# Two block turns of the expert loop written as products in 64-column halves, and a reordered start of the attention stage

## The reference, cut to what matters

```python
x = x + _L0_xattn_ref(ctx_1024, _layernorm(x))     # alignment of x to the context by dynamic time warping
x = x + _L0_ffn_ref(_layernorm(x), gate, W1, b1, W2, b2)   # 16 experts, 3 per row
x = x + _L1_xattn_ref(ctx_1024, _layernorm(x), mask, ...)  # attention over context and x
x = x + _L1_ffn_ref(_layernorm(x), Wg, bg, Wi, Wo, A, B)   # 4 low-rank experts on a shared base
```

```python
hidden = relu(x @ W1[e] + b1[e])        # 512 -> 1024
expert_out = hidden @ W2[e] + b2[e]     # 1024 -> 512
out = sum over the 3 chosen e of gate_topk[e] * expert_out
```

## Time and profile before

| what | us |
|---|---|
| median of 3 runs | 1135.21 |
| lowest and highest run | 1132.46, 1137.16 |
| the profiled execution, its own time | 1130.05 |
| its span | 1128.4 |
| TensorE busy | 1023.9 (91%) |
| first turn_hidden of the loop to the last | 363.66 to 709.69 |
| first seam instruction of TensorE | 720.85 |

### The profile page before, as it was taken

One profiled execution on the slowest core, in us unless ns is written; L12 is line 12 of the kernel. 1 busy time (PEld: TensorE's weight loads), 2 busy tenths in 40 slices (PEclk: granted clock), 3 DMA queues, 4 the chain that ended last, 5 costly groups with the idle time before them and its releaser, 6 DMA issues. The chain is left out here.

```text
span 1128.4 us, 19664 instructions
## 1 busy us (share of the span) xinstructions
PE 1023.9 (91%) x6339; PEld 637.5 (57%) x6340; DVE 521.8 (46%) x2007; ACT 349.0 (31%) x947; POOL 257.5 (23%) x327
## 2 busy tenths in 40 slices
PE   8966679973996999999999999799999989999997
PEld 7963234542465666666666666554466655555553
DVE  6938888885565222222222222457755643112212
ACT  3633765774013222222222222242354420000000
POOL 2773030221002333333333333200030001112111
PEclk9987889995998999999999999899999999999999
DMA  8868004215825486778788675630030022000000
GB/s 306 249 118 296 11 1 150 84 57 140 276 65 172 132 266 186 255 206 266 241 264 268 189 232 177 166 106 1 0 150 1 1 63 106 1 1 1 22 8 30
DMA packets 74701, 148.42 MB, mean 132 GB/s; under 512 B 12946, under 2 KB 24986, under 8 KB 73806
## 3 DMA queue, kind: packets, MB, share of 16 engines
q1 hardware_dynamic: 63750, 129.11, 34.8%
q0 software_dynamic: 9568, 14.69, 6.3%
q10 hardware_dynamic: 1320, 3.84, 1.4%
HBM read 128.29 MB, written 19.33 MB: 131 GB/s over the span
## 5 line engine op out<-in xcount | busy, mean ns | idle before, releaser
L1434 ACT ACTIVATE att<-ba,b 128x64 f32<-128x64 f32 x180 | 41.9, 315 | 215.7 <-PE ba L1343 210.9
L2627 DVE SCALAR_TENSOR_TENSOR tiles<-bf,shared 128x400 f32<-128x400 f32 x64 | 32.4, 567 | 129.9 <-PE bf L2546 129.6
L2561 PE MATMUL acc<-tiles 128*128 128x400 f32 x256 | 90.6, 505 | 0.0
L1329 PE MATMUL ba<-shared,att 128*64 128x256 f32 x736 | 88.4, 382 | 0.0
L1352 PE MATMUL ba<-shared,att 128*64 128x256 f32 x736 | 83.4, 379 | 0.9 <-ACT att L1434 0.9
L1329 PE MATMUL ba<-Wmem,att 128*64 128x256 f32 x672 | 81.1, 383 | 1.7 <-issue 1.2
L1455 DVE TENSOR_TENSOR att<-ba,att 128x256 f32<-128x256 f32 x45 | 19.1, 425 | 134.8 <-PE ba L1352 134.8
L1352 PE MATMUL ba<-Wmem,att 128*64 128x256 f32 x704 | 79.7, 379 | 0.0
L1491 POOL DMA_INDIRECT xg_sb<-xn_d,from_row x46 | 45.7, 993 | 122.9 <-ACT from_row L1419 99.1
L1450 DVE TENSOR_SCALAR att<-ba,b 128x64 f32<-128x64 f32 x180 | 39.2, 278 | 72.9 <-PE ba L1343 72.5
L2520 PE MATMUL bf<-shared,Wmem 128*128 128x400 f32 x192 | 70.0, 501 | 2.3 <-PEq L54 1.6
(11 more groups left out here) (412 smaller groups left out, 1895.6 us busy)
## 6 DMA issues: line engine op xcount, KB each, us to landing
Wmem<-in_W SPq DMA_DIRECT2D x16, 2048.0 KB
shared<-in_W SPq DMA_DIRECT2D x16, 2048.0 KB
cT<-in_ctxT SPq DMA_DIRECT2D x8, 1444.0 KB, 14.0
ctx_rows<-in_ctx SPq DMA_DIRECT2D x8, 1280.0 KB
Wmem<-in_Wkv SPq DMA_DIRECT2D x2, 2048.0 KB, 8.6
tiles<-in_WoT SPq DMA_DIRECT2D x4, 1024.0 KB
Wmem<-in_WiT SPq DMA_DIRECT2D x3, 1024.0 KB, 6.9
cost_mem<-dist SPq DMA_DIRECT2D x8, 330.6 KB, 4.9
```

Source lines behind the costliest of these rows:

```text
L1329: ins = pe.matmul(pa[part][h * Q:(h + 1) * Q, :], xT[:, k, :], w[:, k, h * HH + part * DQ:h * HH + (part + 1) * DQ], start=k == 0, stop=k ...
L1434: act.activation(hT[:, j, :], pt[0][:, n * P + half * Q:n * P + (half + 1) * Q], ACT.Relu, bias=b1[:, bass.ds((e + u) * HJ + j, 1)]).then_ ...
L2561: ins = pe.matmul(acc[k][:, 0:NT4], WoT[:, f, k * P:(k + 1) * P], hs[i % 4][:, :], start=f == 0, stop=f == FJ - 1)
L2627: dve.scalar_tensor_tensor((h1[i % 4], h2[i % 2])[k][:, :], bank[i % NBK][:, 0:NT4], 0.0, wb[k][:, g * NT4:(g + 1) * NT4], ALU.max, ALU.mu ...
```

## The change

`turn_rows` and `turn_hidden` no longer call `pe.transpose`. Each 128 x 128 turn becomes two `pe.matmul` calls: the stationary operand is 64 columns of the source, the moving operand is the 128 x 128 identity, and the output goes to partitions 0 to 63 or 64 to 127. The values in PSUM are the same transposed block. ScalarE gets one more activation, a Sqrt of a column of the identity into an unused slot of `rstd`, in front of root(0). VectorE does normalise(0) directly behind variances(0).

```diff
         def turn_rows(src):
             for m in range(2):
-                ins = pe.transpose(px[:, m * P:(m + 1) * P], src[:, m * P:(m + 1) * P], ident[:, :])
+                for h in range(2):
+                    ins = pe.matmul(px[h * Q:(h + 1) * Q, m * P:(m + 1) * P], src[:, m * P + h * Q:m * P + (h + 1) * Q], ident[:, :],
+                                    start=True, stop=True)
             ins.then_inc(xt_mm, 1)
...
                     q = 2 * i + n
-                    ins = pe.transpose(pt[i][:, n * P:(n + 1) * P], pre[:, q * P:(q + 1) * P], ident[:, :])
+                    for h in range(2):
+                        ins = pe.matmul(pt[i][h * Q:(h + 1) * Q, n * P:(n + 1) * P], pre[:, q * P + h * Q:q * P + (h + 1) * Q],
+                                        ident[:, :], start=True, stop=True)
                 ins.then_inc(t_mm, 1)
...
             expert_act(act)
             full_act(act)
+            act.activation(rstd[:, B - 1:B], ident[0:S, 0:1], ACT.Sqrt)
             root(0)
             root(1)
             keep_T(0)
...
             full_dve(dve)
-            for m in range(B // 2 + 1):
+            variances(0)
+            normalise(0)
+            for m in range(1, B // 2 + 1):
                 if m < B // 2:
                     variances(m)
-                if m:
+                if m > 1:
                     normalise(m - 1)
```

## The result

| | before | after |
|---|---|---|
| median of the runs side by side (4 and 4) | 1133.84 | 1146.22 |
| profiled execution, its span | 1130.05, 1128.4 | 1145.62, 1143.9 |
| ratio of the runs, 95% interval | | 1.0127 [1.0093, 1.0162] |

The two medians lie 12.4 us apart. The ratio of the runs gives +14.4 us, with an interval of 10.5 to 18.4; +14.6 was forecast. The forecast of 1149 lies 3 us above the median of the changed kernel, partly because the runs of before that it started from had a median 1.4 us above the one with the fourth run added.

The account below looks back on a forecast made before the run. TensorE's own queue was taken to bound the expert stage. Turns +15.0 us over 44 chunks, ends +0.2 and seam -0.6 made +14.6; on the median 1135.2 that gave 1149.8, rounded down to 1149, range 1143 to 1156.

Parts of the forecast that it names:

- TensorE's queue alone sets a chunk: Expert stage: TensorE was busy 346.20 of 347.59 us, so a turn's cost there counts in full, times 44 chunks.
- The slot: 0.1086 us: Expert chunk on TensorE: 128 moving columns take 0.1086 us, from 0.836 ns a column and 1.6 ns fixed; at most 0.114.
- Before: 0.65 of slots and 0.31 of form change: Expert chunk before the edit: six transposes cost 0.96 us, 0.65 for six slots and 0.31 for changing the tiling form.
- The three gaps that the prediction names: Around the old chunk's turns: 0.11 us before the first turn, 0.06 more before L1335, 0.10 more before L1329.
- After: two records a call, 12 slots, no gap: Expert chunk after: 12 calls, 24 paired records, 1.30 us for the turns without form change, +0.34 us a chunk.
- One pass: Rival on the turns: each identity product is one record, so -0.31 us a chunk, 1121 us in all; chance 4%.
- Halves not side by side: Rival on the turns: 24 records run one behind another, 2.61 us, +72 us in all, 1207 us; chance 3%.
- coming apart: Rival on the turns: half the slots lose their pairing, 18 slots instead of 12, +44 us, 1179 us; chance 5%.
- The ends: +0.2 us: Stage's two ends: prologue turns +0.2 and -0.1 us, last turn_hidden +0.1; sum +0.2, bounds 0 and 0.6.
- The seam: -0.6 us: Behind the stage: turn(0) gains 1.0 us, keep_T(0) 0.65, value_rows(0) starts 0.6 earlier; span -1.2 to +2.3 us.
- The whole: 1149, and +14.6: Whole kernel: +14.6 us on the median 1135.2 gives 1149.8, rounded down to 1149; slower with 94%.

Follow-up runs that it names:

- two bf16 terms: Each turn as the PSUM sum of two bf16 identity products in halves, seam edits kept, against the kernel before: 1121.11 us, ratio 0.9910.

## Why the prediction was right, point by point

- *TensorE's queue alone sets a chunk.* Held in every kernel with a chunk of 7.86 us or more, where TensorE waits once in the stage, for 0.7 to 0.9 us. At 7.60 its weight loads wait 2.9 us for ScalarE at expert boundaries, and at 7.26 it waits 4.5 us for VectorE.
- *The slot: 0.1086 us.* Measured 1.31 / 12 = 0.109.
- *Before: 0.65 of slots and 0.31 of form change.* Held, by two kernels that move one and not the other: +0.65 for six more transposes, +0.30 for one more change of form. The three gaps that the prediction names sum to 0.27 us (0.11 + 0.06 + 0.10); the rest stands in the L1329 behind, whose 8 slots take 1.77 us and not 1.72. The Trainium skill's page "TensorEngine Tiling (Array Packing)", section "Tiling Modes", says that a change of tiling mode drains TensorE. The trace agrees in that a fixed price is paid, 0.30 us for there and back; that it is a drain no run here shows.
- *After: two records a call, 12 slots, no gap.* Held. The step of +0.34 us a chunk was 0.35 to 0.36 (8.217 - 7.863), the stage +15.4 for +15.0.
- *Rivals.* One pass: its condition was not met, the calls had two records. With one (and with bf16 slots, half as long) the chunk fell to 7.26. The number of records does decide: at the same length of a slot, 12 slots took 0.69 us with two bf16 terms and 6 took 0.35 with one. Halves not side by side, or coming apart: excluded by 24 records (x16 and x8) in 1.31 us. The Trainium skill's page "TensorE: Matmul & The Clock Gate", section "Terms", calls the transpose mode 4 times faster for fp32. The trace does not agree: a turn takes two slots as products and one as a transpose, a factor of 2.
- *The ends: +0.2 us.* The sum came out, its parts did not. The first turn_rows of the prologue cost nothing (0.96 us to the first layer behind it, 0.97 after; +0.2 forecast), the second cost 0.07 and did not save 0.1, and from the last turn_hidden to the second layer it took 1.75 us in place of 1.56 (+0.1 forecast). All this is within what executions differ by.
- *The seam: -0.6 us.* The path held, the size in this execution did not, and a single execution can't show it. The 50 keep_awake records took 8.38 us and not 7.48, since the lower clock level lasted longer (the granted clock was 0.67 from the first of them to turn(0), 0.79 before), so turn(0) gained 0.28 us (741.74 - 733.53 against 8.49) and not 1.0. root(1) was late by itself, at +8.8 and not +8.25, because the stats of batch 3 came 4.70 us after the first (3.54 before), but behind the later turn(0) it took back only 0.06 us and not 0.35. It came to -0.25, and to -0.96 in the kernel with the seam edits alone, where keep_awake took 7.72. The execution that the forecast started from was one of six with the old seam, and these lie 2 us apart.
- *The whole: 1149, and +14.6.* That +14.4 by the ratio comes so near is in part luck. The stage was 0.4 us above its forecast, the two profiled executions differ by 15.5 us in their spans, and the medians by 12.4.

## What to carry to other kernels

Price a turn on TensorE by its slots times their length (with 128 moving columns 0.109 us in fp32, 0.057 in bf16), and add what it costs to leave the array's present form. The form change is paid once a stretch, so a part of such a change can cost more than all of it. An fp32 product with the identity takes two records where the transpose takes one. By an estimate from these prices that outweighs the saved change as soon as three turns stand together (3 x 0.109 = 0.33 extra against 0.30); only six were tried. With bf16 terms the same idea pays, at about 16 of the 24 bits. And compare a stretch of a microsecond over several executions before you give an edit the credit: in the seam the same instructions took between 9.8 and 11.8 us.

## What was not expected of the hardware

In the 64-column form a bf16 pair with 128 moving columns starts every 0.057 us: 0.69 us for 12 slots with two bf16 terms, where only the identity is read at every second 16-bit element, and 0.35 for 6 slots with one record a call, where the stationary operand is read so too. The upper halves of fp32 words could thus be used in place, without a copy, at no visible price.

The table load of ScalarE stands at 727.23, 5.2 us before the activation that it serves (732.42): the wait for `full_over` was carried by the activation, and the load in front of it did not wait with it. Before, a wait for `var_ok` of its own (L1849, at 725.91) stood in front of the load, and the load came behind it, at 725.96.
